# Order of the score matmuls in attention, and four weight tiles in rotation instead of two in the feed-forward stage

## The reference, cut to what matters

```python
x = x + attention(layernorm(x))     # 16 heads, causal
#   scores = q_nope @ k_nope.T + q_rope @ k_rope.T    (128 and 64 wide)
#   softmax over the keys, then @ v, then @ w_o
x = x + ffn(layernorm(x))
#   x1, x2 = x @ quantize(w1).T, x @ quantize(w2).T   (5632 wide)
#   ffn = (sigmoid(x1) * x2) @ quantize(w3).T
# quantize(w) = clip(round(w / (mean(abs(w)) + eps)), -1, 1)
```

## Time and profile before

| | us |
|---|---|
| median of 3 runs | 5444.41 (5441.38 to 5446.41) |
| the profiled execution, its own time | 5453.22 |
| its span on the slowest core (core 1) | 5451.7 |
| spans of the other cores | 5422.4 to 5442.9 |
| TensorE busy | 3972.4 |
| VectorE busy | 2085.7 |
| ScalarE busy | 1309.2 |

### The profile page before, as it was taken

How to read it: one execution, slowest core, us unless ns; L and a number is a source line. 1 busy time by engine, 2 the same in 40 slices (tenths; PEclk the granted TensorE clock), 3 DMA queues, 4 the chain that set the end, 5 groups by cost and what they waited for, 6 DMA issues and landing times. The chain is left out here.

```text
span 5451.7 us, 60255 instructions; the slowest of 8 cores (5422.4 to 5451.7 us)
## 1 busy us (share of the span) xinstructions
PE 3972.4 (73%) x20688; PEld 1912.7 (35%) x20688; DVE 2085.7 (38%) x3835; ACT 1309.2 (24%) x1970; POOL 287.4 (5%) x509
## 2 busy tenths in 40 slices
PE   2936775776677577748737777768887888788879
PEld 1413332333233233313323343333333333333334
DVE  5445556555655655541256666530000000000000
ACT  5202331322222133200166666620000000000000
POOL 0000000000000000000001111101000100010001
PEclk9966565555666655659857887879999999999999
DMA  7012222223122232224358888855344433443444
GB/s 172 16 23 68 93 82 67 81 76 89 58 76 89 57 93 82 78 56 138 148 200 260 266 268 259 265 191 153 128 134 155 154 128 131 155 153 130 132 154 153
DMA packets 270297, 710.24 MB, mean 130 GB/s; under 512 B 27762, under 2 KB 83058, under 8 KB 247988
## 3 DMA queue, kind: packets, MB, share of 16 engines
q1 hardware_dynamic: 198628, 462.56, 26.0%
q0 software_dynamic: 71376, 243.83, 15.5%
HBM read 619.25 MB, written 102.76 MB: 132 GB/s over the span
## 5 line engine op out<-in xcount | busy, mean ns | idle before, releaser
L1374 PE MATMUL e1s_px<-BB,e1s_t 128*128 128x512 bf16 x5632 | 1310.8, 391 | 159.4 <-DMA e1s_t<-w2qT 122.6
L1374 PEld LDWEIGHTS e1s_px<-BB,e1s_t 128*128 128x128 bf16 x5632 | 554.8, 101 | 878.8 <-issue 300.7
L1493 PE MATMUL e2s_pu<-e2s_w,h_sb 128*128 128x512 bf16 x2816 | 627.5, 387 | 102.8 <-DMA e2s_w<-w3qT 81.6
L1337 DVE TENSOR_TENSOR h_sb<-e1s_sg,e1s_px 128x512 bf16<-128x512 f32 x176 | 121.0, 687 | 1240.8 <-PE e1s_px L1374 1240.8
L670 PE MATMUL ps_o<-v_sb,PT_sb 128*128 128x128 bf16 x2176 | 272.2, 306 | 247.7 <-DVE PT_sb L823 247.7
L1493 PEld LDWEIGHTS e2s_pu<-e2s_w,h_sb 128*128 128x128 bf16 x2816 | 279.4, 99 | 451.0 <-issue 131.3
L659 PE MATMUL ps_pt<-idn_sb,P_sb 128*128 128x128 bf16 x2176 | 289.6, 299 | 176.4 <-DVE PT_sb L823 164.1
L1388 PE MATMUL e1s_pwf<-idn_sb,e1s_wq 128*128 128x128 bf16 x2112 | 215.6, 267 | 239.1 <-DVE e1s_t L1330 218.5
L1300 ACT ACTIVATE e1s_sg<-e1s_px 128x512 f32<-128x512 f32 x176 | 105.2, 598 | 1113.8 <-PE e1s_px L1374 1113.8
L1330 DVE CAST e1s_t<-e1s_pwf 128x1024 bf16<-128x1024 f32 x264 | 310.2, 1216 | 64.7 <-DMA w3qT<-e1s_t 64.6
L670 PEld LDWEIGHTS ps_o<-v_sb,PT_sb 128*128 128x128 bf16 x2176 | 212.7, 138 | 304.4 <-issue 304.4
(11 more groups left out here) (170 smaller groups left out, 3603.4 us busy)
## 6 DMA issues: line engine op xcount, KB each, us to landing
gb<-w SPq DMA_DIRECT2D x264, 256.0 KB, 3.1
dump<-w SPq DMA_DIRECT2D x264, 256.0 KB, 3.0
e1s_w<-w SPq DMA_DIRECT2D x66, 1024.0 KB, 8.5
e1s_w<-w POOLq DMA_DIRECT2D x66, 1024.0 KB, 8.4
e1s_t<-w1qT SPq DMA_DIRECT2D x132, 512.0 KB, 3.2
e1s_t<-w2qT POOLq DMA_DIRECT2D x132, 512.0 KB, 3.5
e2s_w<-w3qT POOLq DMA_DIRECT2D x176, 256.0 KB, 3.2
e2s_w<-w3qT SPq DMA_DIRECT2D x176, 256.0 KB, 3.2
```

The lines of the kernel that those rows point to most:

```text
L1374: ins = e.matmul(dst[:, 0:512], wqT[i % 2][:, kc * 128:(kc + 1) * 128], BB3[:, kc, sg * SG:(sg + 1) * SG], start=(kc == 0), stop=(kc == KC ...
L1493: ins = e.matmul(pu[tl * 2 + sub][:, 0:512], h_sb[:, c * 512 + tl * 128: c * 512 + (tl + 1) * 128], w3s[buf(r, c)][:, sub * 512: (sub + 1) ...
```

## The change

There are two edits. In attention, for tiles 8 to 15, all no-position products are issued first (chunks 0 and 1, then the wait for s_ex at 2 * k_g, then the rest), and then all rotary products; the signal to DVE that the first 1024 columns are done comes with the rotary product of chunk 1. For tiles 0 to 7 the order of instructions is the same as before. In E1 of groups 1 to 3 the loads go to four tiles in rotation, wqT and A_sb2, and an item's load waits for the item four before it.

```diff
-                            if qi >= 8:
-                                e.wait_ge(s_ex, 2 * k_g - 1)
-                                parts = [(0, 2), (2, nck)]
...
-                            for pi, (c0, c1) in enumerate(parts):
-                                if pi == 1:
-                                    e.wait_ge(s_ex, 2 * k_g)
-                                for ck in range(c0, c1):
-                                    ... e.matmul(ps_sc, qn_sb, kn_sb)
-                                for ck in range(c0, c1):
-                                    ... ins = e.matmul(ps_sc, qr_sb, KR)
-                                if pi == 0 and len(parts) == 2:
+                            for ck in range(nck):
+                                nn = min(512, klen - ck * 512)
+                                if ck == 0:
+                                    if qi >= 8:
+                                        e.wait_ge(s_ex, 2 * k_g - 1)
...
+                                if ck == 2 and qi >= 8:
+                                    e.wait_ge(s_ex, 2 * k_g)
+                                e.matmul(ps_sc[:, off + ck * 512: ...
+                                         start=True, stop=False)
+                            for ck in range(nck):
+                                ins = e.matmul( ... qr_sb ... KR ... )
+                                if ck == 1 and qi >= 8:
                                     ins.then_inc(s_sc, 1)
...
-                if i >= 2:
-                    xdone_wait(e, i - 2)
-                ins = e.dma_start(wqT[i % 2][:, :], wt_hbm[m].ap()[c, :, :])
+                if i >= 4:
+                    xdone_wait(e, i - 4)
+                dstb = (wqT + A_sb2)[i % 4]
+                ins = e.dma_start(dstb[:, :], wt_hbm[m].ap()[c, :, :])
...
                     if sg == 0:
                         s_wtv.w(e, 2 * (i + 1))
+                        lhs = wqT[i % 2]
                     else:
                         wref(e, loadref[i])
+                        lhs = (wqT + A_sb2)[i % 4]
...
-                            wqT[i % 2][:, kc * 128:(kc + 1) * 128],
+                            lhs[:, kc * 128:(kc + 1) * 128],
```

More of the change, by code:

```diff
@@ L766, in _ @@
                             nck = (klen + 511) // 512
-                            if qi >= 8:
-                                e.wait_ge(s_ex, 2 * k_g - 1)
-                                parts = [(0, 2), (2, nck)]
[L770 to L774, removed]
-                                    e.wait_ge(s_ex, 2 * k_g)
-                                parts = [(0, nck)]
@@ new lines, in _ @@
+                            for ck in range(nck):
[3 more added lines that the diff above has]
+                                        e.wait_ge(s_ex, 2 * k_g - 1)
+                                    elif 1 <= qi <= 7:
+                                        if k_g >= 2:
+                                            e.wait_ge(s_ex, 2 * (k_g - 1))
+                                    elif k_g >= 1:
+                                        e.wait_ge(s_ex, 2 * k_g)
+                                if ck == 2 and qi >= 8:
+                                    e.wait_ge(s_ex, 2 * k_g)
+                                e.matmul(ps_sc[:, off + ck * 512:
+                                               off + ck * 512 + nn],
+                                         qn_sb[:, qi * 128:(qi + 1) * 128],
+                                         kn_sb[:, ck * 512:ck * 512 + nn],
+                                         start=True, stop=False)
@@ new lines, in _ @@
+                            for ck in range(nck):
+                                nn = min(512, klen - ck * 512)
+                                diag = (ck == nck - 1)
+                                ins = e.matmul(
+                                    ps_sc[:, off + ck * 512:
+                                          off + ck * 512 + nn],
+                                    qr_sb[:, qi * 128:(qi + 1) * 128],
+                                    KR[:, ck * 512:ck * 512 + nn],
+                                    start=False, stop=not diag)
+                                if ck == 1 and qi >= 8:
```

## The result

The change makes the kernel faster: 5319.7 us (median of 9 runs, 5313.1 to 5341.8) against 5444.4 us for the kernel before (7 runs), measured beside it: 124.7 us less. The ratio is 0.9771, with a 95% interval of 0.9752 to 0.979. Forecast were 5323 us. (In some executions of most kernels here the cores of a die are granted less clock and the time is up to 8% longer; such runs are left out of all times and ratios, and where a profiled execution was touched in attention, only the cores of the other die are compared.) The profiled execution took 5319.7 us, 133.5 less than the one before, and its slowest core is core 0. The new kernel's lines are numbered a little lower: L1374 is now L1372, L922 is L917, L927 is L922, L932 is L927, L782 is L779, L792 is L787, L800 is L795.

A forecast was written before the change was run, and what follows sets the result against it. E1 of groups 1 to 3 was taken as bound by w2 load latency, attention's late steps by a TensorE-DVE chain. Edit B -143 and edit A +22 give -121 us: 5332 from the profiled 5453.2, 5323 against the median; range 5285 to 5362.

The forecast's parts named there:

- 0.16 us of matmul tail a gap: E1, groups 1 to 3: gap time beyond the shown waits, 129 x 0.16 = 21 us saved by edit B.
- d: Attention, edit A: later start of the first-half maximum, 0.107 us per 128 second-half keys, 3.84 us a head.
- 0.23 us for two changes of height: Attention, edit A: two fewer operand-height changes a step, 0.11 us each, end the mask product 0.22 us earlier.
- 1.14 us to the second maximum: Attention, edit A: the second-half maximum starts 1.14 us after the first's start in all eight steps.
- 8 us more for the steps at the upper level: Attention, edit A: 25 of 128 steps taken as high-clock cost 8 us beyond the low-clock sum of 14 us.
- no change in how many those are: Attention, edit A: the number of high-clock steps was taken as unchanged, 0 us.
- the bounds of 20 us: Attention clock: losing all 25 high-clock steps at 0.8 us costs +20 us; as many more give -20 us.
- That A costs nothing or gives: Rival, attention: mask product's end sets the step, edit A 0 to -28 us, total 5273 to 5301; chance 0.10.
- the row on which it stood: Attention timeline: a 0.427 us matmul takes 0.54 us at an operand-height change, so 0.11 us each; 28 us saved.
- That A costs more: Rival, attention: full delay paid and high-clock stretches lost, +61 + 20 us, total 5350 to 5382; chance 0.10.
- That B gives only half: Rival, E1: loads stay late with twice as many in flight, 72 us gained, total 5395 us; chance 0.05.
- That a denser TensorE is granted less: Rival, E1 groups 1 to 3: gapless matmuls get less clock, total about 5535 to 5551 us; chance 0.03.

The follow-up runs named there:

- b_three: Edit B with three tiles in rotation instead of four, attention as in the kernel before: 5310 us, ratio 0.974 to the kernel before.
- two_sp: Kernel before, two tiles in rotation, but all loads of E1's groups 1 to 3 issued by SP instead of every second one by POOL: 5387 us.
- b_filled: Edit B, attention in the old order, plus idle matmuls while TensorE waits for DVE: 5020 us, ratio 0.921 to the kernel before.
- wide_after: Changed kernel (both edits) with the rotary operands widened from 64 to 128 rows with zeros: 5208 us, ratio 0.956 to the kernel before.
- after_filled: Changed kernel (both edits) plus idle matmuls while TensorE waits for DVE: 5062 us, ratio 0.929 to the kernel before.
- wide_rot: Edit B, attention in the old order, rotary operands widened from 64 to 128 rows with zeros: 5172 us, ratio 0.950 to the kernel before.
- fill_narrow: As filled, but the idle matmuls have operands 64 rows high, same columns and count: 5225 us, ratio 0.960 to the kernel before.
- a_alone: Only edit A on the kernel before, E1 unchanged: 5474 us, ratio 1.003 to the kernel before.
- rot_first: Edit B, attention in the old order except rotary products ahead of no-position ones in the second half: 5309 us, ratio 0.976 to the kernel before.
- b_alone: Only edit B on the kernel before, attention unchanged: 5308 us, ratio 0.974 to the kernel before.
- filled: As rot_first, plus idle 512-column matmuls while TensorE waits for DVE in attention: 5044 us, ratio 0.926 to the kernel before.
- wide_filled: Edit B, old attention order, rotary operands widened to 128 rows, plus idle matmuls in the waits: 4991 us, ratio 0.916 to the kernel before.

## Why the prediction was right

**Edit B.** Forecast -143 us; measured -145.2 us in the three stages (-143.5 as a mean over the cores) and 0.974 by itself. Each step held: landings of at most 6.4 us against over 10 us of room, 6.91 us a pair, 0.16 us of matmul tail a gap, granted clock 1.00 at 99.5% busy. b_three shows that the cause is the room for one load, two_sp that POOL's longer issue is the smaller part of the gap and not its root.

**Edit A.** The sign was right, and in attention the size was off by half: forecast +22 us, measured +11 (both edits) and +14 (alone), while the whole kernel's times say 12 to 25 and cannot tell. The parts were right: d, 0.23 us for two changes of height, 1.14 us to the second maximum in every step, and step by step the lengths at the lower level, which were forecast to add up to 14 us. The terms that were mis-sized are those of the clock: 8 us more for the steps at the upper level, and no change in how many those are. There are more of them now. The mask product stands nearer to the first maximum than the lower level allows in 30 of 128 steps before and in 39 now (means over the cores); with 768 and 1024 keys in the second half it is 7 and 10 of 16 before, 14 and 13 now. At 0.8 us a step, nine more give back 7 us, an estimate from the earlier trace rows, and the rest of the missing 8 to 11 us stays open. The 0.8 us is itself the price of a step in which the clock came up part of the way: steps of 768 keys take 8.46 us at the lower level and 6.21 at the upper (b_filled), so the bounds of 20 us were narrow. wide_after and after_filled show the price when the clock has less to give: 35 and 49 us. Why the new order is granted more is open: it puts all the 128-row products behind the value products, which are 128 rows high too, and in wide_rot and fill_narrow the higher operands went with the higher clock. That was not tried by itself.

**The total.** That the forecast of 5323 us came within 4 us is in part luck. The two profiled executions differ by 133.5 us (E1 -145.2, attention +11), where -121 was forecast; the one before, from which the forecast was counted down, lay 8.8 us above its median, the one after on its median, so the medians differ by 124.7.

**The rivals.** That A costs nothing or gives: refuted by a_alone and wide_after; but the row on which it stood is real, and rot_first turns it into a gain of 20 us. That A costs more: true only where the clock is up anyway (35 and 49 us). That B gives only half: refuted by the waits, which are gone. That a denser TensorE is granted less: refuted by the stretches at 1.00 for this execution, in which none of the eight cores shows a level but the two. It is not refuted for every execution. In b_alone's, cores 2 and 3 took 341 us for E1 of group 3, the other six 305 to 307; this is core 2:
```profile
4860.00:4960.00 100.00, 99.38 (x375) 41.44 (x381) 8.26 (x12) 7.17 (x12) 6.34 (x12) 0.81 0.40 126
```
Its granted clock is 0.81. So such a loss exists, but for 5535 us it would have to come in every execution. The Trainium skill (TensorE: Matmul & The Clock Gate, Part 1) gives 13/16 of the clock for a die on which three or more cores run dense matmuls. The trace agrees with it on those two cores, and does not in the changed kernel's profiled execution: 1.00 at 99.5% busy. On the changes of height, the Trainium skill (TensorEngine Tiling (Array Packing), Key Properties) says that a change of tiling mode drains TensorE. The trace agrees: 0.11 us a change, gone in wide_rot.

## What to carry to other kernels

If an engine waits a little for every load, compare the room that the rotation leaves (the work time of the tiles in between) with the longest landing, not with the median; one more tile is worth the whole of the gaps, further ones nothing. In a chain between TensorE and DVE the order of products should serve the first instruction that DVE can start, and only then save changes of operand height; rotary-first in the second half did both. Where TensorE waits for another engine and the granted clock is near 0.5, look at the clock before the order: filling the waits with idle 128-row matmuls was worth 237 us here, twenty times edit A in attention.

## What the runs showed of the hardware

The clock granted to TensorE in attention rose from 0.60 to between 0.71 and 0.73 when the rotary operands went from 64 to 128 rows with zeros, at the same count of columns, and to 0.87 or 0.88 with 128-row fillers in the waits, but only to 0.67 to 0.71 with 64-row ones, with which TensorE was busy for longer. In both cases the changes of operand height differ too, and the two were not taken apart. What the level is worth shows in steps that kept one throughout: with 768 keys in the second half 8.46 us at 0.50 (before) and 6.21 us at 1.00 (b_filled and filled), though L922 takes 1.22 to 1.23 us at either. A third level, 0.81, appears in some executions on some cores, in E1 of b_alone for one. Fuller work in attention did not lower the clock later: wide_filled has 9 tenths or more in its last 13 slices, as the kernel before.
